# Rows of B put into PSUM by matmuls, and u*B shared out anew between three engines

## The reference, cut to what matters

```
dbc = xs @ x_proj_w.T
dt = softplus(dbc[..., :16] @ dt_proj_w.T + dt_proj_b)
Bm, Cm = dbc[..., 16:32], dbc[..., 32:]
dA  = exp(dt[..., None] * A)
dBu = dt[..., None] * Bm[:, :, None, :] * xs[..., None]
hs  = scan over the sequence of  h = dA * h + dBu
y = einsum('blds,bls->bld', hs, Cm) + xs * Dvec
y = (y * silu(z)) @ out_proj_w.T
```

## Time and profile before

| | us |
|---|---|
| median of 3 runs | 621.7 (620.38 to 626.72) |
| the profiled execution | 619.76, its span 618.0 |
| the first scan starts | 280.44 |
| the last scan starts | 483.4 |
| DVE busy | 494.6 (80%) |
| PE busy | 481.5 (78%) |
| ACT busy | 317.6 (51%) |
| POOL busy | 260.1 (42%) |

### The profile page before, as it was taken

How to read it: one execution, slowest core, us unless ns; L and a number is a source line. 1 busy time by engine, 2 the same in 40 slices (tenths; PEclk the granted TensorE clock), 3 DMA queues, 4 the chain that set the end, 5 groups by cost and what they waited for, 6 DMA issues and landing times.

```text
span 618.0 us, 7482 instructions
## 1 busy us (share of the span) xinstructions
PE 481.5 (78%) x2695; PEld 317.6 (51%) x2695; DVE 494.6 (80%) x808; ACT 317.6 (51%) x514; POOL 260.1 (42%) x177
## 2 busy tenths in 40 slices
PE   2896999996998989979896988789889969823200
PEld 2255888895987874327352444356344637522200
DVE  3999986987299751675969999899999795499997
ACT  1542311526133425896878888889779223522210
POOL 5152000000000000045668798798888347777003
PEclk9997558999599998995889899999899985655555
DMA  7510000000000001612869789698878000021000
GB/s 196 128 31 1 0 2 3 2 11 1 1 1 10 9 20 30 202 36 88 274 190 314 229 301 309 236 300 266 287 269 263 11 15 9 9 8 8 2 1 34
DMA packets 32470, 63.40 MB, mean 103 GB/s; under 512 B 15952, under 2 KB 18288, under 8 KB 32112
## 3 DMA queue, kind: packets, MB, share of 16 engines
q1 hardware_dynamic: 30640, 62.34, 31.3%
q0 software_dynamic: 1792, 0.58, 1.6%
HBM read 61.14 MB, written 1.77 MB: 102 GB/s over the span
## 4 chain that ended last, share of the span: by engine, by line
DVE 42%; PE 36%; ACT 8%; issue 7%; POOL 6%; DMA 1%; DVEq 0%; SPq 0%; ACTq 0%; POOLq 0%
DVE arena L1663 8%; PE ps L702 8%; PE ps L885 6%; POOL arena L578 5%; DVE arena L1475 4%; PE ps L751 3%; PE ps L724 3%; DVE arena L1848 3%; DVE g L1850 3%; DVE ps L1651 2%; PE ps L991 2%; PE ps L859 2%; PE ps L687 2%; PE ps L1004 2%; PE ps L844 1%
## 5 line engine op out<-in xcount | busy, mean ns | idle before, releaser
L1663 DVE TENSOR_TENSOR_SCAN arena<-arena,ps 128x1024 f32<-128x1024 f32 x64 | 143.8, 2277 | 17.7 <-ACT ps L1207 9.0
L885 PE MATMUL ps<-arena,ident 128*128 128x512 f32 x256 | 128.0, 635 | 14.5 <-POOL arena L578 14.3
L578 POOL TENSOR_TENSOR arena<-arena 128x1024 f32<-128x1024 f32 x48 | 112.8, 2364 | 38.8 <-DVE arena L1663 20.5
L885 PEld LDWEIGHTS ps<-arena,ident 128*128 128x128 f32 x256 | 47.5, 201 | 67.1 <-issue 40.2
L702 PE MATMUL ps<-arena 128*128 128x64 f32 x576 | 77.3, 301 | 2.2 <-DVE x_tok L1392 2.2
L702 PEld LDWEIGHTS ps<-arena 128*128 128x128 f32 x576 | 76.6, 218 | 2.8 <-ACT arena L1065 2.8
L583 POOL MEMSET arena<- 64x24 f32 (+1 forms) x2 | 0.3, 132 | 175.5 <-PE ps L716 175.4
L1152 ACT ACTIVATE arena<-arena,neg_a 128x1020 f32<-128x1020 f32 x64 | 71.2, 1135 | 0.5 <-DVE arena L1663 0.2
L631 POOL DMA_INDIRECT arena<-node_rows,src_idx x56 | 55.5, 991 | 31.8 <-issue 16.8
L1065 ACT ACTIVATE arena<-ps 128x768 f32<-128x768 f32 x48 | 37.4, 809 | 44.0 <-PE ps L751 43.9
L1190 ACT ACTIVATE arena<-arena,b_col 128x128 f32<-128x128 f32 x192 | 58.3, 387 | 0.0
(11 more groups left out here) (345 smaller groups left out, 761.1 us busy)
## 6 DMA issues: line engine op xcount, KB each, us to landing
arena<-state_rows SPq DMA_DIRECT2D x88, 512.0 KB, 4.9
cs<-state_rows SPq DMA_DIRECT2D x16, 512.0 KB, 4.9
arena<-dram_edges SPq DMA_DIRECT2D x2, 1024.0 KB, 8.7
arena<-dram_x SPq DMA_DIRECT2D x2, 512.0 KB, 4.6
arena<-node_rows,src_idx POOLq DMA_INDIRECT x56, 2.7
x_tok<-dram_x SPq DMA_DIRECT2D x1, 512.0 KB, 10.9
res_scratch<-x_tok SPq DMA_DIRECT2D x4, 128.0 KB, 2.0
arena<-res_scratch SPq DMA_DIRECT2D x1, 512.0 KB, 3.3
```

Of the source, the lines that this page charges most:

```text
L578: g.tensor_tensor(gg[n % 2], hh[n % 2], cs[n % GROUP], ALU.mult).then_inc(s["g_ready"], 1)
L885: m = pe.matmul(ps[:, 4 + q, :], ident[:], gg[n % 2][:, 512 * q:512 * q + 512], start=False, stop=True, skip_group_check=True)
L1663: v.tensor_tensor_scan(o, x0, x1, 0.0, ALU.mult, ALU.add).then_inc(s["scan_ready"], 1)
```

## The change

POOL and ACT no longer take a row of B from DRAM. Both directions' rows of B and C stay in SBUF in one tile, `rows` (partitions 0 to 31 forward, 32 to 63 backward), and only C's rows still go through DRAM. Where DVE multiplies, PE's new `put_b(n)` writes the broadcast row into PSUM: a float32 matmul whose weights are one column of the identity repeated 128 times (16 rows for forward, 48 for backward), with 512 tokens as the moving operand, twice.

The 64 steps are shared out anew. DVE multiplies in 25 (n % 16 in 0, 3, 5, 8, 11, 13, but 0, 1, 2, 5, 8, 11, 13 in the first block), POOL in 4 (n % 16 = 10), with its product in the tiles with tokens on partitions, and ACT in the other 35. The 39 of ACT and POOL are turned back by PE. hh, da and ub get a third buffer each, and the waits on them move by one step. B's columns are transposed from `rows` in place of a matmul with xs. The diff, cut to its core:

```diff
-TURN = 8
-TURNED = TURN // 2 - 1
+DVE_STATES = [n for n in range(STATES) if n % DS in (0, 3, 5, 8, 11, 13) and n != 3 or n in (1, 2)]
+POOL_STATES = [n for n in range(STATES) if n % DS == 10]
+ACT_STATES = [n for n in range(STATES) if n not in DVE_STATES and n not in POOL_STATES]
+TURNED = sorted(ACT_STATES + POOL_STATES)
...
-def turned(n):
-
-    return n // TURN * TURNED + n % TURN // 2 - 1
+def parts_by(n):
+
+    done = sum(m <= n + 2 for m in ACT_STATES)
+    return min(2 * len(ACT_STATES), 2 * done)
...
+            def own_b(n):
+
+                blk, at = n // DS, TURNED.index(n)
+                g.wait_ge(s["ub_put"], at - 2)
+                g.wait_ge(s["ut_ready"], blk + 1)
+                g.wait_ge(s["bt_ready"], blk // 2 + 1)
+                q0 = blk % 2 * (HALF // P)
+                g.tensor_tensor(ub[at % 3].rearrange("p (q c) -> p q c", c=P), u_tok[blk].rearrange("p (q c) -> p q c", c=P),
+                                b_col[blk // 2][:, q0:q0 + HALF // P, n % DS:n % DS + 1].to_broadcast([P, HALF // P, P]), ALU.mult).then_inc(s["ub2_ready"], 1)
...
-                g.tensor_tensor(gg[n % 2], hh[n % 2], cs[n % GROUP], ALU.mult).then_inc(s["g_ready"], 1)
+                g.tensor_tensor(gg[n % 2], hh[n % 3], cs[n % GROUP], ALU.mult).then_inc(s["g_ready"], 1)
...
+                if n + 4 in POOL_STATES:
+                    own_b(n + 4)
...
+                pe.wait_ge(s["rows_kept"], 2 * d + 2)
+                k, wide = 2 * DS * (d + 1), 16 // (d + 1)
                 for t in range(NT):
-                    m = pe.matmul(ps[:, bank, DS * t:DS * t + DS], xs[d][:, P * t:P * t + P], xp_w[d][:, 0:DS], start=True, stop=True)
+                    m = pe.transpose(ps[:, bank + t // wide, k * (t % wide):k * (t % wide) + k], rows[0:k, P * t:P * t + P], ident[0:k, 0:k])
                 m.then_inc(s["bt_psum"], 1)
+
+            def put_b(n):
+
+                d, c0, bank = n // (2 * DS), n // DS % 2 * HALF, 6 * (n % 2)
+                k, at = DS + 2 * DS * d, 2 * DS * d + n % DS
+                if n > 1:
+                    pe.wait_ge(s["scan_ready"], n + 1)
+                for q in range(2):
+                    m = pe.matmul(ps[:, bank + q, :], ident[0:k, at:at + 1].to_broadcast([k, P]), rows[0:k, c0 + 512 * q:c0 + 512 * q + 512],
+                                  start=True, stop=True)
+                m.then_inc(s["b_put"], 1)
...
+                at, bank = TURNED.index(n), 6 * (n % 2)
+                if n in POOL_STATES:
+                    pe.wait_ge(s["ub2_ready"], POOL_STATES.index(n) + 1)
+                else:
+                    pe.wait_ge(s["ub_ready"], ACT_STATES.index(n) + 1)
                 pe.wait_ge(s["scan_ready"], n + 1)
                 for q in range(HALF // P):
-                    m = pe.transpose(ps[:, 6 + q // 4, P * (q % 4):P * (q % 4) + P], ub[a % 2][:, P * q:P * q + P], ident[:])
+                    m = pe.transpose(ps[:, bank + q // 4, P * (q % 4):P * (q % 4) + P], ub[at % 3][:, P * q:P * q + P], ident[:])
                 m.then_inc(s["ub_put"], 1)
...
+            pe.wait_ge(s["z_ready"], 1)
+            put_b(0)
             pe.wait_ge(s["z_ready"], 2)
             turn_u(0)
             pe.wait_ge(s["z_ready"], 3)
             b_columns(0, 4)
             pe.wait_ge(s["z_ready"], 4)
+            put_b(1)
             pe.wait_ge(s["diag_ready"], 2)
             pe.wait_ge(s["rest_t_ready"], 1)
             for n in range(STATES):
                 blk, i = n // DS, n % DS
                 if n == 2 * DS:
                     pe.wait_ge(s["ut_ready"], 4)
-                if n % 2 and n % TURN > 1:
+                if n in TURNED:
                     turn_back(n)
+                elif n > 1:
+                    put_b(n)
...
             def decay(n):
 
                 d, c0, lo = n // (2 * DS), n // DS % 2 * HALF, 1 - n // (2 * DS)
-                act.wait_ge(s["scan_ready"], n + 1)
-                f(da[n % 2].rearrange("p (b s) -> p b s", s=SEQ)[:, :, lo:lo + SEQ - 1],
+                if n >= 3:
+                    act.wait_ge(s["scan_ready"], n)
+                if n // 3 == 2 * DS // 3 or n // 3 == 2 * DS // 3 + 1:
+                    act.wait_ge(s["da_zero"], min(max(n - 2 * DS + 4, 3), 6))
+                f(da[n % 3].rearrange("p (b s) -> p b s", s=SEQ)[:, :, lo:lo + SEQ - 1],
                   dtv[d][:, c0:c0 + HALF].rearrange("p (b s) -> p b s", s=SEQ)[:, :, lo:lo + SEQ - 1], ACT.Exp,
                   scale=neg_a[d][:, n % DS:n % DS + 1]).then_inc(s["da_ready"], 1)
...
-            def put_b(n):
-
-                m = n // 2
-                act.wait_ge(s[f"bd_in{m % 2}"], 16 * (m // 2) + 16)
-                act.wait_ge(s["scan_ready"], n + 1)
-                f(banks(0, 2), bd[m % 2], ACT.Copy).then_inc(s["b_put"], 1)
...
+            def with_b(n, part):
+
+                blk, at = n // DS, TURNED.index(n)
+                if part == 0:
+                    if at >= 3:
+                        act.wait_ge(s["ub_put"], at - 2)
+                    else:
+                        act.wait_ge(s["dt_ready"], 2)
+                    act.wait_ge(s["ut_ready"], blk + 1)
+                    act.wait_ge(s["bt_ready"], blk // 2 + 1)
+                for q in range(4 * part, 4 * part + 4):
+                    m = f(ub[at % 3][:, P * q:P * q + P], u_tok[blk][:, P * q:P * q + P], ACT.Copy,
                           scale=b_col[blk // 2][:, (blk % 2) * (HALF // P) + q, n % DS:n % DS + 1])
-                m.then_inc(s["ub_ready"], 1)
...
+                if part:
+                    m.then_inc(s["ub_ready"], 1)
+
+            def columns_read(d, bank):
+                wide = 16 // (d + 1)
+                act.wait_ge(s["bt_psum"], d + 1)
+                for b in range(d + 1):
+                    m = f(b_col[d][:, wide * b:wide * b + wide, :],
+                          ps[:, bank + b, :].rearrange("p (t n) -> p t n", t=wide)[:, :, 2 * DS * d:2 * DS * d + DS], ACT.Copy)
+                m.then_inc(s["bt_ready"], 1)
+
+            u_copy(0)
+            columns_read(0, 4)
+            act.wait_ge(s["dt_ready"], 2)
+            done = 0
+            for n in range(2, STATES):
+                decay(n)
+                if n in TURN_U_AT:
                     u_copy(TURN_U_AT.index(n) + 1)
                     if n == TURN_U_AT[0]:
-                        act.wait_ge(s["bt_psum"], 2)
-                        f(b_col[1][:].rearrange("p t n -> p (t n)"), ps[:, 2, 0:NT * DS], ACT.Copy).then_inc(s["bt_ready"], 1)
-                if n % 2 and (n + 2) % TURN > 1 and n + 2 < STATES:
-                    with_b(n + 2)
+                        columns_read(1, 2)
+                while done < parts_by(n):
+                    with_b(ACT_STATES[done // 2], done % 2)
+                    done += 1
             f(pause[:, 3:4], ident[:, 0:1], ACT.Sqrt)
...
             def scan_state(n):
-                d, c0, e = n // (2 * DS), n // DS % 2 * HALF, n % 2
-                b = banks(6 * e, 2)
-                if e == 0:
-                    v.wait_ge(s["b_put"], n // 2 + 1)
+                d, c0, e = n // (2 * DS), n // DS % 2 * HALF, n % 3
+                b = banks(6 * (n % 2), 2)
+                if n in DVE_STATES:
+                    at = DVE_STATES.index(n) + 1
+                    v.wait_ge(s["b_put"], at)
                     tt(b, uu[d][:, c0:c0 + HALF], b, ALU.mult).then_inc(s["b_made"], 1)
+                    v.wait_ge(s["b_made"], at)
+                else:
+                    v.wait_ge(s["ub_put"], TURNED.index(n) + 1)
                 v.wait_ge(s["da_ready"], n + 1)
-                v.wait_ge(s["g_ready"], n + 1)
-                if e == 0:
-                    v.wait_ge(s["b_made"], n // 2 + 1)
-                elif n % TURN > 1:
-                    v.wait_ge(s["ub_put"], turned(n) + 1)
-                else:
-                    v.wait_ge(s["bx_put"], n // TURN + 1)
+                if n >= 3:
+                    v.wait_ge(s["g_ready"], n)
                 o, x0, x1 = hh[e], da[e], b
```

More of the change, by code:

```diff
@@ L53 @@
 J_GROUP = [0] * 6 + [1] * 6 + [2] * 4
-WMAMBA = 2 * 6 * 16
+WMAMBA = 13 * 16
 HID = 2 * C
@@ L266, in program @@
         xs, zs, dtv, uu = ([ar(T)] for _ in range(4))
-        bd = [ar(HALF) for _ in range(2)]
+        rows = ar(T, parts=4 * DS)
+        state_rows = [rows[2 * DS * d:2 * DS * d + 2 * DS] for d in range(2)]
         wg_t = cw_b[0].rearrange("p k c -> p (k c)")[0:HE, 0:2 * C]
@@ L347, in program @@
         nb_t = br(ROW * WC_MAX)
-        ub = [br(HALF) for _ in range(2)]
+        ub += [br(HALF) for _ in range(2)]
         u_tok.append(br(HALF))
```

101 lines of the change are left out of this document (21 added, 80 removed).

## The result

The changed kernel is slower: 639.13 us, median of 4 (636.29 to 641.64), beside 621.04 for the kernel before on the same chip. The ratio is 1.028 [1.019, 1.036]. The profiled execution took 640.46 us, with a span of 638.7.

The account below looks back on a forecast made before the run. DVE was full before; PE was taken to become the bound. Its sum ended the turn of state 63 at 491.0, 10 us behind 480.97, making 630 from the profiled 619.8, so 631 as a median; range 611 to 643.

Parts of the forecast that it names:

- PE full, DVE waiting for it: Scan loop: PE over 97% busy from state 5 on, DVE's idle time ended by PE's puts and turns.
- DVE stays the bound: Rival for the scan loop: scan 63 near 460, some 600 us in all; needs puts of 0.3 us; chance 0.13.
- The price of a put, 1.72: PE's float32 matmuls that put a row of B into PSUM: 1.72 us each, as an add of a state.
- The upper bound: Price of a put on PE: 2.5 us if each of four weight loads of 0.20 us stood by itself.
- The start, 295.5: From put 0 to PE's turn of state 4: ends at 295.5 us, on a clock that rises.
- The second rival: Whole kernel: gains and losses cancel, 615 to 626 us, a never idle PE keeping full clock; chance 0.18.
- States 5 to 31 at 87.9: PE's sum for the rest of the first half: adds, 10 puts, turns and backward columns take 87.9 us, to 383.4.
- States 32 to 47 at 54.7: PE's sum for the third block of 16 states: 54.7 us, to 438.1, where these took 48.0 before.
- States 48 to 63 at 52.9: PE's sum for the last 16 states: 15 adds, backward products, 6 puts, 10 turns and skip take 52.9 us, to 491.0.
- Behind it the order is as before: After PE's turn of state 63: same order as before, so its 10 us delay passes to the kernel's end.
- Nothing for ACT, POOL and transfers: Scan loop: ACT's added copies, POOL's fewer products and 40 dropped broadcast transfers are worth nothing.
- More transposes and the clock: Rival for PE's clock: turns go from 10% to 16% of the stage, clock falls, 650 us; chance 0.09 shared with another.

Follow-up runs that it names:

- Full height: The changed kernel with every put reading all 128 partitions of the rows tile, not 16 or 48 rows: 632.8 us, ratio 1.010 to the kernel before.

## Why the prediction was right, and where it was short

The forecast was the mechanism that happened: PE became the bound, and its sum set the end. 631 was 8.1 us short of 639.13, inside the range of 611 to 643, but above the 626 to 638 that the forecast had by itself. The sum itself was further off: it ended the turn of state 63 at 491.0, and that turn ended at 504.00. Step by step:

- **PE full, DVE waiting for it.** Right: PE 204.4 of 206 us, DVE's 34.6 us of waits for puts. *DVE stays the bound* needed a put of 0.3 us, and fell with 1.91. DVE had been able to go faster, as the run without puts shows (loop 198.1).
- **The price of a put, 1.72.** Mis-sized, for a reason that the prediction did not have. Inside a run of one height the price was right, by the puts twice (1.71). What came on top is the change of height, 0.19 us at each edge; 22 puts from state 5 on x 0.38 is 8.4 us. The upper bound, four loads of 0.20 that stand by themselves, had the right cause and the wrong count: one load at each edge. The earlier trace rows was misread: its four matmuls over 16 rows took 1.22 us at a granted clock of 0.50 (231 to 233 us), so they are no price at full clock, and they stood between weights of 128 rows. Their first weight load began with the first matmul, at 231.85, and not ahead of it, so the trace of before held a sign of the edge.
- **The start, 295.5.** Mis-sized by 5.2 us, the largest single miss (300.69). I let the clock rise behind put 0. It stayed at 1.2 GHz for 24 us. Full height gives 16.5 us for this piece, close to my 18.4. The second rival's line, that a PE which never idles keeps the full clock from the start on, does not hold: behind put 0 PE had no gap and stayed at 1.2 GHz, and with the puts twice the clock fell with no gap at all.
- **States 5 to 31 at 87.9.** They took 91.3 (300.69 to 392.00, the ends of the turns of states 4 and 31). Ten puts make 3.8 of it and the fall at 385.01 1.8; cheaper adds and turns take back 1.0, and the backward columns, priced at 4.0 with PE's wait, took 2.4 (the turn of u ends near 316.1, the next turn starts at 318.52).
- **States 32 to 47 at 54.7.** They took 55.9 (to 447.89, the end of the turn of state 47). Six puts with their edges make 2.3 more than I had; adds and turns at 1.72 and 0.87 and not 1.74 and 0.90 give 0.6 back, and one of my 18 products stands in the next piece (0.3).
- **States 48 to 63 at 52.9.** They took 56.1 (to 504.00), 3.2 more. My sum has 15 adds; the list has 16 between the turns of states 47 and 63, so one add, 1.8, was left out. The puts with their edges make 2.3 and the product of the third block 0.4; 1.3 came back, half of it because adds beside backward products cost 1.81 behind a turn (500.88 to 502.69) and not 1.87. The rest I did not trace.
- **Behind it the order is as before.** The order is, but not the time. Before, scan 63 started 2.4 us behind its turn (480.97 to 483.4), because DVE had scan 62 to do; now DVE waits for the turn, and scan 63 starts at 504.20. The changed kernel won 2.3 us here.
- **The two halves.** From first scan to last, the second half (scan 32 to scan 63) became 14.1 us longer (397.09 to 504.20, before 390.44 to 483.4), as the 12 to 14 forecast. The first half, forecast to be a little shorter, became 5.7 longer, by the start and the puts' edges.
- **Nothing for ACT, POOL and transfers.** Right in the main: PE is full, and what they hold up on DVE is small beside the 34.6 for puts. One wait of 3.1 us is for a decay that ACT makes behind its read of the backward columns. The third buffers, called cover and no more, were right for this kernel, where DVE is not the bound. The run with two buffers shows them worth 6.3 us of loop (204.4 against 198.1) where it is.
- **More transposes and the clock.** Not seen: the stretch from 388 to 486 has some 150 transposes and a clock of 1.00.

The terms measured against those said: 5.2 for the start, 3.4 for states 5 to 31, 1.2 and 3.2 behind, 13.0 together, less the 2.3 behind state 63. That is the 10.7 between 629.8, the sum before rounding, and the profiled 640.46. Every piece of the loop took longer than said, none shorter.

What stays open is why the clock is lower with puts of 16 rows. "TensorE: Matmul & The Clock Gate" in the Trainium skill, part 1, says that the chip sets the clock by how busy PE has been. The busy time of the profile does not show that here: from 278 to 298 PE was busy 4.00 of every 4 us at 0.50, and with the puts twice 114.00 of 114 us at 0.91. What the runs show is that the height of the puts' weights makes a difference. Whether 48 rows do less than 128 is open too: in the changed kernel the 48-row stretches kept 1.00, and with the puts twice one fall came there. And the clock falls in some stretches of the kernel before as well, so rows are not all there is to it.
